# The bias of the output projection moved from a TensorE product with a row of ones to an add on GpSimd

## The chip, the cores and the metric

One Trainium2 chip, of which the kernel uses one core. The time is device microseconds of one execution. Engines are named as in the profile: PE is TensorE (PEld its weight loads), DVE is VectorE, ACT is ScalarE, POOL is GpSimd, SP is SyncE, which here only issues DMAs; PEq, SPq and so on are the engines' own queues.

## What is computed

A graph attention layer over 6250 nodes of 512 features and 100,000 edges (sorted by destination row), then a small feed-forward network, both with a residual. Cut to what matters here:

```python
edge_index = jnp.stack([src, dst])
x = x + _L0_gnn_ref(_layernorm(x), edge_index, edge_attr_8, Wq, bq, Wk, bk, Wv, bv, Wo, bo)
x = x + _L0_ffn_ref(_layernorm(x)[None], Wa, ba, Ws, bs)[0]

# in _L0_gnn_ref
q = (x @ Wq + bq).reshape(n, H, DK); k = (x @ Wk + bk)...; v = (x @ Wv + bv)...
logits = einsum('ehd,ehd->eh', q[rows] * scale, k[cols]) + att_bias
p = exp(logits - row_max[rows]);  att = p / denom[rows]
y = segment_sum(att[:, :, None] * v[cols], rows)
out = y.reshape(n, H * DK) @ Wo + bo
```

The feed-forward network reads a few thresholded features of each node (two rows of four numbers), sends them through two stacks of three layers of width 160, and adds rounded results into 33 of the 512 columns.

## The kernel before, in words

The nodes are cut into W = 49 windows of 128 rows (the last has 106). The work goes through stages in this order: the edges are read, turned into rows and counted per window (a histogram by products on PE), beside it q, k and v of the windows are computed and written to DRAM; the edges are sorted into tiles by scatter DMAs (POOL, L548); k rows are gathered for the logits (POOL, L561); v rows are gathered and summed per window (POOL, L571; PE L1661; DVE L1270); and last, per window, the result is normalized, projected, added to x, and sent through the feed-forward network. Each engine has its own instruction stream, written out by hand as nested functions in its block, and engines meet only through semaphores. The order on an engine is the order of the program text: there is no planner.

**The biases at the start.** SP loads bq, bk and bv as 32x16 pieces (L373) and bo (L374), then 38 small weights of the network (L382). DVE splits each bias into three bfloat16 terms whose sum is the float32 value (`split_bias`, L889 to L897), called at L916 and L917 for the two groups. SP copies the terms into rows on three partitions: nine DMAs for q, k, v (L403) and three for bo into `boS` (L407). The products of q, k and v on PE (L1530) each end with a product of a 3x128 tile of ones and those rows (L1533), which adds the bias in PSUM. Before the first of them PE waits for all twelve copies (L1532). Histogram products (L1541) and these units stand in one PE queue.

**The last stage.** SP loads Wo (L498) when the v stage is over, then x again for the first eight windows, into a ring of XR = 8 tiles `xr` (`f_load`, L503), and later stores pair g-1 and loads pair g+3 (`f_store`, L509). A load waits for the store that used its tile before. Windows are handled in pairs, g = 0 to 24. For each window:
- DVE `f_y` divides by the softmax sums (L1304 to L1311); PE `f_yT` transposes (L1683); ACT `f_yTe` copies (L752).
- PE `f_wo` makes four products of 128x512 with Wo (L1695) and ends with ones times `boS` (L1697), all into one PSUM bank.
- DVE `f_x1` adds the bank to x in place (L1318), after waiting for the product and for the load of x; `f_stats` takes mean and variance (L1325 to L1333), with a root on ACT (L783, `f_root`); `f_feats` writes the normalized row xn (L1356, L1363) and then some 14 small operations that end with the features as bfloat16 parts (L1368 to L1424).
- POOL `f_xs` adds xn to x in place (L577); this is all that POOL does in this stage.
- PE `f_fq` transposes the features (L1707), ACT copies them (L763); the layers are `f_h1` (L1715, ReLU on ACT L771), `f_h2` (L1725, ReLU L778) and `f_out` (L1739), which has four columns per product and runs 24 of them per pair.
- DVE `f_posts` (L1442 to L1475) rounds and adds into x, and SP stores.

The PE order of a pair stands at the end of the block. `f_wo` is called with a range of its five steps (0 to 3 the Wo products, 4 the bias), so that those steps of the pair after next stand between the layers of this pair: for the first window (0,1), (1,3), (3,5) behind the three parts of `f_h1`, for the second (0,2) behind `f_h2`, then `f_fq` of the next pair, and (2,3), (3,4), (4,5) behind the first three of four `f_out` parts. Every product in float32 runs as two instructions in the profile. On DVE the order in pair g is x1, statistics, posts of g-1, features of g+1, and `f_y` of g+4.

Of the kernel before, what the change touches and what calls it, by code (L numbers as in the profile page):

```python
# [17 lines left out]
def build(nc, x, src, dst, attr, wq, bq, wk, bk, wv, bv, wo, bo, waT, ba, wsT, bs, out):  # L18
# [4 lines left out]
    W = 49  # L23
# [18 lines left out]
    with ctx:  # L42
# [67 lines left out]
        Bt = [ar(3 * 48, bf16).rearrange("p (r n) -> p r n", r=3) for _ in range(2)]  # L110
        Bf = [ar(48) for _ in range(2)]
        Br = [ar(48) for _ in range(2)]
# [26 lines left out]
        boS = f_(512, bf16)  # L139
# [165 lines left out]
        w16 = e_(64).rearrange("p (a n) -> p a n", a=4)  # L305
        G = (W + 1) // 2
        s_ftz, s_wo = sem("s_ftz"), sem("s_wo")
        s_xt = sems("s_xt", XR // 2)
# [18 lines left out]
        def _(e):  # L327
# [44 lines left out]
            for i, b_ in enumerate((bq, bk, bv)):  # L372
                e.dma_start(Bf[0][0:32, 16 * i:16 * i + 16], b_.rearrange("(p n) -> p n", n=16)).then_inc(s_bl, 16)  # L373
            e.dma_start(Bf[1][0:32, 0:16], bo.rearrange("(p n) -> p n", n=16)).then_inc(s_bl, 16)  # L374
# [26 lines left out]
            for i in range(3):  # L401
                for j in range(3):
                    e.dma_start(Bs[i:i + 1, 512 * j:512 * j + 512].rearrange("a (p n) -> a p n", n=16),  # L403
                                Bt[0][0:32, i, 16 * j:16 * j + 16]).then_inc(s_brow, 16)
            q.wait_ge(s_bv, 8)
            for i in range(3):
                e.dma_start(boS[i:i + 1, 0:512].rearrange("a (p n) -> a p n", n=16), Bt[1][0:32, i, 0:16]).then_inc(s_brow, 16)  # L407
# [90 lines left out]
            e.dma_start(WoS, wo.rearrange("(c p) n -> p c n", p=128)).then_inc(s_wo, 16)  # L498

# [26 lines left out]
        def _(e):  # L526
# [52 lines left out]
            for w in range(W):  # L579
                f_xs(w)  # L580
# [232 lines left out]
        def _(e):  # L813
# [75 lines left out]
            def split_bias(k, n, bf, br, bt):  # L889

                e.tensor_copy(bt[0:32, 0, 0:n], bf[0:32, 0:n]).then_inc(s_bv, 1)
                q.wait_ge(s_bv, 4 * k + 1)
                e.tensor_tensor(br[0:32, 0:n], bf[0:32, 0:n], bt[0:32, 0, 0:n], ALU.subtract).then_inc(s_bv, 1)
                q.wait_ge(s_bv, 4 * k + 2)
                e.tensor_copy(bt[0:32, 1, 0:n], br[0:32, 0:n]).then_inc(s_bv, 1)
                q.wait_ge(s_bv, 4 * k + 3)
                e.tensor_tensor(bt[0:32, 2, 0:n], br[0:32, 0:n], bt[0:32, 1, 0:n], ALU.subtract).then_inc(s_bv, 1)  # L897
# [11 lines left out]
            for c in range(NCH + AHEAD):  # L909
                if c == 12:  # L910
                    e.memset(stV[:, :, 64:65], 1.0).then_inc(s_cv, 1)
                if c == 32:
                    ln_stats(0)
                    ln_out(0)
                    q.wait_ge(s_bl, 64)
                    split_bias(0, 48, Bf[0], Br[0], Bt[0])  # L916
                    split_bias(1, 16, Bf[1], Br[1], Bt[1])  # L917
# [396 lines left out]
            def f_x1(w):  # L1314
                n, k, xx = rows_of[w], w % 2, xr[w % XR]
                q.wait_ge(s_fo, w + 1)
                q.wait_ge(s_xt[w // 2 % 4], 32 * (w // XR) + 16 * len(pair(w // 2)))
# [183 lines left out]
        def _(e):  # L1501
# [9 lines left out]
            def unit(u):  # L1511
# [20 lines left out]
                q.wait_ge(s_brow, 12 * 16)  # L1532
# [154 lines left out]
            def f_wo(w, c0=0, c1=5):  # L1687
# [3 lines left out]
                q.wait_ge(s_brow, 12 * 16)  # L1691
                q.wait_ge(s_x1, w - 1)
                for c in range(c0, c1):
                    if c < 4:
                        e.matmul(BK[1 + k][0:n, :], yT[w % 4][:, c, 0:n], WoS[:, c, :], start=(c == 0), stop=False)  # L1695
                    else:
                        e.matmul(BK[1 + k][0:n, :], ones[0:3, 0:n], boS[0:3, :], start=False, stop=True).then_inc(s_fo, 1)  # L1697
# [59 lines left out]
            for g in range(G):  # L1757
# [5 lines left out]
                if n2:  # L1763
                    f_wo(n2[0], 1, 3)
                f_h1(g, 2)
                if n2:
                    f_wo(n2[0], 3, 5)
# [7 lines left out]
                if len(n2) > 1:  # L1775
                    f_wo(n2[1], 0, 2)
# [3 lines left out]
                if len(n2) > 1:  # L1780
                    f_wo(n2[1], 2, 3)
                f_out(g, (1,))
                if len(n2) > 1:
                    f_wo(n2[1], 3, 4)
                f_out(g, (2,))
                if len(n2) > 1:
                    f_wo(n2[1], 4, 5)
# [28 lines left out]
```

## Time and profile before

| what | value |
|---|---|
| median of 3 runs | 3968.57 us (3964.55 to 3970.23) |
| profiled execution | 3972.73 us, span 3970.9 us |
| granted clock of PE, mean over the span | 0.929 |
| busy: PE, DVE, POOL, ACT | 82%, 77%, 64%, 40% |
| the last stage | 3392 to 3971 us |
| L1697, product with ones, in the last stage | 49, one of 128x512 drawn with 385 ns |
| L577, add on POOL | 49, mean 1382 ns |

Times are microseconds from the start of the span. A row of a timeline has the start, the length, the engine, the line of the kernel, the operation, the tiles (R, fw, small are large tiles of SBUF, banks is PSUM) and the count of instructions put together; in brackets stands how long the engine had been idle before it and who released it. PE's products overlap and their ends are modelled, so the step from one start to the next says what a product costs. The granted clock is a fraction of full speed: 1.00 is 2.4 GHz, 0.50 is 1.2 GHz. "issue" is a wait for nothing that the profile shows.

### The profile page before, as it was taken

Reading aid. Unit: us, or ns where it says so; the run is one execution under the profiler, and the core shown is the slowest. Engines: PE = TensorE matmul, PEld = TensorE weight load, DVE = VectorE, ACT = ScalarE, POOL = GpSimd, SP = SyncE. Lnnn points to the kernel's source line nnn. Section 1 sums busy time; section 2 is a strip of 40 time slices with the busy share of each in tenths; the row PEclk is TensorE's granted clock in tenths of the full one; section 3 lists DMA queues with packets and bytes.
Section 4 is the critical chain, followed back from the end, with each engine's and each line's share of the span. In section 5 each row is a group of like instructions: output and inputs, shape, how many; then the busy total and the mean of one; then the engine's idle time right before and its main releaser. Section 6 shows DMA issues by size and latency. Waiting matters only on the chain. (4 is left out here: it accounts for less than half of the span.)

```text
span 3970.9 us, 46880 instructions
## 1 busy us (share of the span) xinstructions
PE 3251.2 (82%) x12499; PEld 1740.2 (44%) x12499; DVE 3046.2 (77%) x7930; ACT 1569.7 (40%) x3864; POOL 2531.8 (64%) x2586
## 2 busy tenths in 40 slices
PE   5799898888824777777777688888888888899998
PEld 3455454444411222222222266665566655344443
DVE  7676666666625999999999888888888888565654
ACT  4443333333302222222222267777677776222222
POOL 4377777777775777777777777777777777011110
PEclk8899898888957999999999989999999999899998
DMA  5243343333337777777777868888888788211111
GB/s 146 80 128 113 97 112 104 100 105 101 102 117 240 233 241 235 235 237 237 238 237 238 211 200 229 238 235 235 229 231 234 234 235 204 68 48 43 53 43 37
DMA packets 280166, 663.66 MB, mean 167 GB/s; under 512 B 85022, under 2 KB 88934, under 8 KB 279652
## 3 DMA queue, kind: packets, MB, share of 16 engines
q0 software_dynamic: 158144, 443.78, 39.4%
q1 hardware_dynamic: 115416, 204.10, 16.3%
q10 hardware_dynamic: 6348, 12.80, 0.9%
q8 instruction: 106, 1.74, 0.2%
q14 instruction: 152, 1.25, 0.1%
HBM read 599.96 MB, written 60.50 MB: 166 GB/s over the span
## 5 line engine op out<-in xcount | busy, mean ns | idle before, releaser
L1661 PE MATMUL banks<-R,small 128*128 128x260 f32 x3328 | 894.4, 408 | 156.3 <-DVE R L1257 138.0
L571 POOL DMA_INDIRECT R<-v_scratch,dstS x832 | 829.2, 997 | 262.0 <-issue 159.7
L561 POOL DMA_INDIRECT R<-k_scratch,dstS x832 | 791.9, 952 | 291.1 <-issue 261.3
L548 POOL DMA_INDIRECT rec_scratch<-R,small x782 | 770.5, 985 | 282.9 <-issue 237.4
L1603 PE MATMUL banks<-R,small 128*128 x1664 | 799.5, 614 | 184.9 <-DVE R L1114 149.2
L1661 PEld LDWEIGHTS banks<-R,small 128*128 128x128 f32 x3328 | 593.4, 195 | 404.3 <-DVE R L1257 313.4
L731 ACT ACTIVATE R<-R 128x65 f32<-128x65 f32 x2496 | 663.1, 339 | 268.3 <-DMA R<-v_scratch,dstS 263.7
L1530 PE MATMUL banks<-R 128*128 128x512 f32 (+1 forms) x1176 | 610.9, 668 | 62.0 <-ACT R L597 61.8
L1270 DVE TENSOR_TENSOR R<-R,banks 128x520 f32 x832 | 571.2, 686 | 24.2 <-PE banks L1661 18.3
L1603 PEld LDWEIGHTS banks<-R,small 128*128 128x128 f32 x1664 | 292.2, 191 | 653.1 <-issue 653.1
L1114 DVE TENSOR_TENSOR R<-banks,R 128x1024 f32<-128x1024 f32 x416 | 503.8, 1211 | 79.8 <-DMA R<-k_scratch,dstS 43.1
L1121 DVE TENSOR_REDUCE R<-R 128x16 f32<-128x1024 f32 x416 | 502.1, 1207 | 0.0
L1257 DVE TENSOR_TENSOR R<-R 128x325 f32<-128x325 f32 x832 | 407.0, 489 | 108.2 <-DMA R<-v_scratch,dstS 106.2
L686 ACT ACTIVATE small<-rowR,npidx 128x1024 f32<-128x1024 bf16 x104 | 119.5, 1149 | 804.1 <-PE banks L1603 776.6
L1530 PEld LDWEIGHTS banks<-R 128*128 128x128 f32 (+1 forms) x1176 | 239.4, 214 | 321.5 <-issue 254.8
L577 POOL TENSOR_TENSOR R<-R 128x512 f32<-128x512 f32 (+1 forms) x49 | 66.8, 1380 | 491.4 <-DVE R L1363 491.4
L608 ACT ACTIVATE R<-banks 128x512 f32<-128x512 f32 (+1 forms) x147 | 87.9, 598 | 554.3 <-PE banks L1533 554.3
L1003 DVE SCALAR_TENSOR_TENSOR R<-R 128x128 f32<-128x128 uint16 x782 | 268.1, 344 | 7.8 <-DMA R<-src_rows 7.8
L1565 PE MATMUL banks<-R 128*128 128x49 f32 x1564 | 208.4, 302 | 68.2 <-issue 38.3
L1043 DVE SCALAR_TENSOR_TENSOR small<-R 128x8 int32<-128x8 f32 x98 | 16.3, 167 | 309.4 <-DMA rec_scratch<-R,small 309.4
L1695 PE MATMUL banks<-R 128*128 128x512 f32 (+1 forms) x392 | 232.6, 704 | 3.0 <-DMA R<-in_L_gnn_Wo_dram 1.6
L1565 PEld LDWEIGHTS banks<-R 128*128 128x128 f32 x1564 | 195.1, 203 | 88.5 <-issue 56.5
(226 smaller groups left out, 3228.1 us busy)
## 6 DMA issues: line engine op xcount, KB each, us to landing
rowR<-lo_sorted SPq DMA_DIRECT2D x104, 512.0 KB, 5.8
rowR<-lo_rows SPq DMA_DIRECT2D x97, 256.0 KB, 3.9
R<-src_rows SPq DMA_DIRECT2D x97, 256.0 KB
R<-in_x_dram SPq DMA_DIRECT2D x96, 256.0 KB, 2.9
R<-k_scratch,dstS POOLq DMA_INDIRECT x832, 3.9
R<-v_scratch,dstS POOLq DMA_INDIRECT x832, 3.9
rec_scratch<-R,small POOLq DMA_INDIRECT x782
v_scratch<-R SPq DMA_DIRECT2D x48, 260.0 KB
```

The costliest lines, as they stand in the source:

```text
L548: e.indirect_dma_start(recd, bass.IndirectOffsetOnAxis(ap=ridx[:, c % 4, j:j + 1], axis=0), rec[:, 8 * c + j, :], None).then_inc(s_sc[c % ...
L561: e.indirect_dma_start(Kr[t // 2 % (KR // 2)][:, 512 * (t % 2):512 * (t % 2) + 512], None, Kd, bass.IndirectOffsetOnAxis(ap=dstS[:, t:t + ...
L571: e.indirect_dma_start(Vr[t % VR], None, Vd, bass.IndirectOffsetOnAxis(ap=dstS[:, t:t + 1], axis=0)).then_inc(s_v2[t % VR], 16)
L731: ins = e.activation(heads(Vr[t % VR], h, h + 1), heads(Vr[t % VR], h, h + 1), ACT.Copy, scale=ph[:, h:h + 1])
L1114: e.tensor_tensor(Kr[i % (KR // 2)], QB[i % 3], Kr[i % (KR // 2)], ALU.mult).then_inc(s_pr, 1)
L1121: e.tensor_reduce(flat(Lr[k][:, 2 * (i % 8):2 * (i % 8) + 2, :]), Kr[i % (KR // 2)].rearrange("p (h d) -> p h d", d=64), AX.X, ALU.add).th ...
L1257: e.tensor_tensor(heads(Vr[t % VR], 0, HA2), heads(Vr[t % VR], 0, HA2), ph[:, 0:HA2].rearrange("p (h a) -> p h a", a=1).broadcast_to([128, ...
L1270: e.tensor_tensor(yw, yw, YB[t % 3].rearrange("p (q n) -> p q n", q=2)[:, :, 0:260], ALU.add).then_inc(s_ya, 1)
L1530: e.matmul(bank[0:n, :], xT[w % 2][:, c, 0:n], W3[m][:, c, :], start=(c == 0), stop=False)
L1565: ins = e.matmul(BK[GK[c % 3]][:, j * W:(j + 1) * W], AT[c % 3][:, j, :], Cs[c % 3][:, :, j], start=True, stop=True)
L1603: e.matmul(QB[t // 2 % 3][:, 512 * (t % 2):512 * (t % 2) + 512], ohT[(t // 8) % 2][:, t % 8, :], Qall[:, bass.ds(e.snap(win[t % 16], min_v ...
L1661: ins = e.matmul(YB[t % 3][:, 512 * i:512 * i + 260], o, Vr[t % VR][:, 260 * i:260 * i + 260], start=True, stop=True)
```

## The change

The product of ones and `boS` goes from `f_wo`, and with it the load, the split and the three copies of bo. The bias is loaded once in the last stage, spread over 128 partitions, into `boB`, a part of the tile `small` that is free by then; SP issues this DMA between Wo and the loads of x. POOL adds `boB` to each x tile (`f_xb`) as soon as the load has landed, two pairs ahead in its own order: the adds of pair 0, then for each g those of pair g+1 followed by `f_xs` of pair g. `f_x1` on DVE waits for that add instead of the load. `f_wo` has four steps, and its calls in the loop are cut anew. PE's wait before the first product of q, k, v is for nine copies. The tiles `Bt`, `Bf`, `Br` are one each, so that what is carved behind them in R2 lies 168 words lower.

```diff
-        Bt = [ar(3 * 48, bf16).rearrange("p (r n) -> p r n", r=3) for _ in range(2)]
-        Bf = [ar(48) for _ in range(2)]
-        Br = [ar(48) for _ in range(2)]
+        Bt = ar(3 * 48, bf16).rearrange("p (r n) -> p r n", r=3)
+        Bf = ar(48)
+        Br = ar(48)
...
-        boS = f_(512, bf16)
...
+        boB = small[:, 512:1024]
+        s_bo, s_xb = s_bl, s_bv
...
-            e.dma_start(Bf[1][0:32, 0:16], bo.rearrange("(p n) -> p n", n=16)).then_inc(s_bl, 16)
...
-            q.wait_ge(s_bv, 8)
-            for i in range(3):
-                e.dma_start(boS[i:i + 1, 0:512].rearrange("a (p n) -> a p n", n=16), Bt[1][0:32, i, 0:16]).then_inc(s_brow, 16)
...
             e.dma_start(WoS, wo.rearrange("(c p) n -> p c n", p=128)).then_inc(s_wo, 16)
+            e.dma_start(boB, bo.rearrange("(a n) -> a n", a=1).broadcast_to([128, 512])).then_inc(s_bo, 16)
...
-            for w in range(W):
-                f_xs(w)
+            def f_xb(w):
+
+                n = rows_of[w]
+                q.wait_ge(s_bo, 48 + 16)
+                q.wait_ge(s_xt[w // 2 % 4], 32 * (w // XR) + 16 * len(pair(w // 2)))
+                e.tensor_tensor(xr[w % XR][0:n, :], xr[w % XR][0:n, :], boB[0:n, :], ALU.add).then_inc(s_xb, 1)
+
+            for w in pair(0):
+                f_xb(w)
+            for g in range(G):
+                for w in pair(g + 1):
+                    f_xb(w)
+                for w in pair(g):
+                    f_xs(w)
...
-                    split_bias(0, 48, Bf[0], Br[0], Bt[0])
-                    split_bias(1, 16, Bf[1], Br[1], Bt[1])
+                    q.wait_ge(s_bl, 48)
+                    split_bias()
...
-                q.wait_ge(s_xt[w // 2 % 4], 32 * (w // XR) + 16 * len(pair(w // 2)))
+                q.wait_ge(s_xb, 4 + w + 1)
                 e.tensor_tensor(xx[0:n, :], xx[0:n, :], BK[1 + k][0:n, :], ALU.add).then_inc(s_x1, 1)
...
-                q.wait_ge(s_brow, 12 * 16)
+                q.wait_ge(s_brow, 9 * 16)
...
-            def f_wo(w, c0=0, c1=5):
+            def f_wo(w, c0=0, c1=4):
...
-                q.wait_ge(s_brow, 12 * 16)
                 q.wait_ge(s_x1, w - 1)
                 for c in range(c0, c1):
-                    if c < 4:
-                        e.matmul(BK[1 + k][0:n, :], yT[w % 4][:, c, 0:n], WoS[:, c, :], start=(c == 0), stop=False)
-                    else:
-                        e.matmul(BK[1 + k][0:n, :], ones[0:3, 0:n], boS[0:3, :], start=False, stop=True).then_inc(s_fo, 1)
+                    ins = e.matmul(BK[1 + k][0:n, :], yT[w % 4][:, c, 0:n], WoS[:, c, :], start=(c == 0), stop=(c == 3))
+                if c1 == 4:
+                    ins.then_inc(s_fo, 1)
...
                 if n2:
-                    f_wo(n2[0], 1, 3)
+                    f_wo(n2[0], 1, 2)
                 f_h1(g, 2)
                 if n2:
-                    f_wo(n2[0], 3, 5)
+                    f_wo(n2[0], 2, 4)
...
                 if len(n2) > 1:
-                    f_wo(n2[1], 0, 2)
+                    f_wo(n2[1], 0, 1)
                 if n1:
                     f_fq(g + 1)
                 f_out(g, (0,))
                 if len(n2) > 1:
-                    f_wo(n2[1], 2, 3)
+                    f_wo(n2[1], 1, 2)
                 f_out(g, (1,))
                 if len(n2) > 1:
-                    f_wo(n2[1], 3, 4)
+                    f_wo(n2[1], 2, 3)
                 f_out(g, (2,))
                 if len(n2) > 1:
-                    f_wo(n2[1], 4, 5)
+                    f_wo(n2[1], 3, 4)
                 f_out(g, (3,))
```

## Rows read from the trace of the kernel before

**Rows 1.** Busy time of TensorE over the span, from the page.
```profile
PE 3251.2 (82%) x12499; PEld 1740.2 (44%) x12499; DVE 3046.2 (77%) x7930; ACT 1569.7 (40%) x3864; POOL 2531.8 (64%) x2586
```

**Rows 2.** Window of 20 pairs: length, PE, PEld, DVE, ACT, POOL, clock, DMA.
```profile
3439.40:3886.20 446.80, 446.80 (x1422) 192.33 (x1422) 266.67 (x1317) 120.08 (x240) 54.62 (x40) 0.94 0.14 48
```

**Rows 3.** Waits, 3400 to 3900 us: us in total, times, longest.
```profile
DVE R L1318 <- PE banks L1697: 140.5, 21, 7.7
...
PE banks L1683 <- ACT R L752: 1.5, 2, 0.8
```

**Rows 4.** Timeline of PE, one pair at full clock: start, length, what.
```profile
3663.64 0.40 PE L1707 MATMUL banks<-small,R 128*36 128x128 bf16 x4
...
3668.24 0.38 PE L1697 MATMUL banks<-fw,ones 3*128 3x512 bf16 x1
3668.56 0.92 PE L1739 MATMUL banks<-fw,R 128*128 128x4 f32 x6
...
3684.60 0.40 PE L1707 MATMUL banks<-small,R 128*36 128x128 bf16 x4
```

**Rows 5.** Timeline of PE: where a pair begins, five of 25 times.
```profile
3439.44 0.40 PE L1707 MATMUL banks<-small,R 128*36 128x128 bf16 x4
...
3462.06 0.40 PE L1707 MATMUL banks<-small,R 128*36 128x128 bf16 x4
...
3486.21 0.40 PE L1707 MATMUL banks<-small,R 128*36 128x128 bf16 x4
...
3507.17 0.40 PE L1707 MATMUL banks<-small,R 128*36 128x128 bf16 x4
...
3886.18 0.40 PE L1707 MATMUL banks<-small,R 128*36 128x128 bf16 x4
```

**Rows 6.** Two windows of that stage (columns as in Rows 2).
```profile
3639.40:3645.00 5.60, 5.60 (x33) 4.14 (x32) 0.53 (x1) 0.63 (x2) 0.00 (x0) 1.00 0.00 0
3645.00:3651.80 6.80, 6.80 (x10) 2.18 (x10) 4.18 (x25) 1.38 (x2) 0.00 (x0) 0.50 0.21 80
```

**Rows 7.** Timeline of DVE in the pair of Rows 4, and at the end.
```profile
3674.18 0.26 DVE L1356 RECIPROCAL small<-small 128x1 f32<-128x1 f32 x2 [0.80 <-ACT small L783]
...
3675.30 2.51 DVE L1368 SCALAR_TENSOR_TENSOR R<-R 128x64 f32<-128x64 f32 x2
...
3680.02 0.28 DVE L1424 TENSOR_TENSOR R<-R 128x24 bf16<-128x24 f32 x2
...
3932.39 0.23 DVE L1368 SCALAR_TENSOR_TENSOR R<-R 106x64 f32<-106x64 f32 x1
3932.53 1.23 DVE L1372 TENSOR_SCALAR R<-R 106x3 f32<-106x3 f32 x1
```

**Rows 8.** Timeline of POOL, SP's queue and ACT in that pair.
```profile
3675.01 2.72 POOL L577 TENSOR_TENSOR R<-R 128x512 f32<-128x512 f32 x2 [18.21 <-DVE R L1363]
...
3673.28 0.82 SPq L509 DMA_DIRECT2D out_dram<-R  x2
3675.99 0.81 SPq L503 DMA_DIRECT2D R<-in_x_dram  x2
...
3682.80 0.68 ACT L778 ACTIVATE R<-banks,fw 64x512 f32<-64x512 f32 x1 [2.27 <-PE banks L1725]
```

**Rows 9.** Start of the stage: DVE's last features, PE's first transposes.
```profile
3419.53 0.28 DVE L1424 TENSOR_TENSOR R<-R 128x24 bf16<-128x24 f32 x2
...
3421.29 0.40 PE L1707 MATMUL banks<-small,R 128*36 128x128 bf16 x4
```

**Rows 10.** Start of the kernel: SP's queue, PE's first row-of-ones product.
```profile
32.46 0.42 SPq L374 DMA_DIRECT2D R<-in_L_gnn_bo_dram  x1
...
59.62 5.70 SPq L403 DMA_DIRECT2D R<-R  x9
65.36 1.85 SPq L407 DMA_DIRECT2D fw<-R  x3
...
68.47 0.58 PE L1533 MATMUL banks<-R,ones 3*128 3x512 bf16 x1 [9.10 <-DMA fw<-R]
```

More of the change, by code:

```diff
@@ L372, in _ @@
             for i, b_ in enumerate((bq, bk, bv)):
-                e.dma_start(Bf[0][0:32, 16 * i:16 * i + 16], b_.rearrange("(p n) -> p n", n=16)).then_inc(s_bl, 16)
-            e.dma_start(Bf[1][0:32, 0:16], bo.rearrange("(p n) -> p n", n=16)).then_inc(s_bl, 16)
+                e.dma_start(Bf[0:32, 16 * i:16 * i + 16], b_.rearrange("(p n) -> p n", n=16)).then_inc(s_bl, 16)
             q.wait_ge(s_iota, 5)
@@ L403, in _ @@
                     e.dma_start(Bs[i:i + 1, 512 * j:512 * j + 512].rearrange("a (p n) -> a p n", n=16),
-                                Bt[0][0:32, i, 16 * j:16 * j + 16]).then_inc(s_brow, 16)
-            q.wait_ge(s_bv, 8)
-            for i in range(3):
-                e.dma_start(boS[i:i + 1, 0:512].rearrange("a (p n) -> a p n", n=16), Bt[1][0:32, i, 0:16]).then_inc(s_brow, 16)
+                                Bt[0:32, i, 16 * j:16 * j + 16]).then_inc(s_brow, 16)
             for k_ in range(NCH):
@@ L887, in unit, with split_bias @@
                     ln_out(w + 1)
[L889 to L897, printed above, removed]
+            def split_bias():
+                e.tensor_copy(Bt[0:32, 0, :], Bf[0:32, :]).then_inc(s_bv, 1)
+                q.wait_ge(s_bv, 1)
+                e.tensor_tensor(Br[0:32, :], Bf[0:32, :], Bt[0:32, 0, :], ALU.subtract).then_inc(s_bv, 1)
+                q.wait_ge(s_bv, 2)
+                e.tensor_copy(Bt[0:32, 1, :], Br[0:32, :]).then_inc(s_bv, 1)
+                q.wait_ge(s_bv, 3)
+                e.tensor_tensor(Bt[0:32, 2, :], Br[0:32, :], Bt[0:32, 1, :], ALU.subtract).then_inc(s_bv, 1)
             def build_A(c, sm_):
@@ L914, in _ @@
                     ln_out(0)
-                    q.wait_ge(s_bl, 64)
-                    split_bias(0, 48, Bf[0], Br[0], Bt[0])
-                    split_bias(1, 16, Bf[1], Br[1], Bt[1])
+                    q.wait_ge(s_bl, 48)
+                    split_bias()
                 if c < NCH:
```

## Prediction, made before the changed kernel ran

> **What bounds the kernel now.** I began with the page: TensorE is the busiest engine at 82% [rows 1], but that is an average over stages with different limits, so the stages that the change touches have to be read one by one. They are two: the last stage, from about 3392 us, where the output projection is computed, and the first 70 us, where the bias is split and copied. Between them the gathers run, which the change leaves alone.
>
> In the last stage the windows view shows PE busy for all of 446.80 us while it goes through 20 pairs of windows; DVE is busy for 60% of that, POOL for 12% [rows 2]. The list of waits agrees: DVE waits 140.5 us for PE's row-of-ones product, and the longest sum that PE itself waits for anybody is 1.5 us [rows 3]. So the stage costs what PE's queue costs.
>
> The PE timeline gives the price of one pair. From one L1707 to the next, at full clock, it is 20.96 us (3663.64 to 3684.60); the product with the row of ones starts at 3668.24 and the next instruction at 3668.56, so it takes 0.32 us of the queue, and not the 0.38 that it is drawn with [rows 4]. The starts of L1707 also show that pairs are not all alike: 22.62, then 24.15, then 20.96 [rows 5]. Of the 20, nine are of 20.96, five of about 22.6, six of about 24.2, together 446.74. The windows view says why. Between 3639.4 and 3645.0 PE runs the transposes of features and 24 four-column products, with two Wo products and one bias product between them, all at clock 1.00; behind it, from 3645.0 to 3651.8, the granted clock is 0.50, the lower of its two levels, 1.2 GHz instead of 2.4, on products of full width [rows 6]. It then returns to 1.00. Over the 20 pairs these falls cost 446.7 - 20 x 20.96 = 27.5 us. Each of the falls follows such a run of small products.
>
> **The change part by part.**
>
> *The product goes.* 49 row-of-ones products by 0.32 us [rows 4] are 15.7 us, all on the queue that bounds the stage. A little is unsafe: a run of Wo products at the place of the bias also saves the change of shape, so up to 0.4 us each, 19.6; the low end is nothing for those in the first pairs. I take 15.7. What could come late in its place are the ACT copies that PE needs; each has at least as many PE instructions in front of it as before except the last ReLU of the second layer, which is left with one Wo product and the four transposes of L1707, more than 1 us together, over an ACT operation of 0.68 us [rows 8]. That covers it.
>
> [...]
>
> *The Wo products are spread anew.* The second window of a pair now has one product ahead of L1707 instead of two, and three between the four groups of small products instead of two and the bias. At full clock that is neutral. But it puts a full-width product where the clock falls from: 24 small products now have three wide ones among them, and nothing thin. In the run of rows 6 PE then has half as much wide work again. The price at one end is nothing, if the clock falls as before; at the other all of the 27.5 us [rows 5, 6], with every pair at 20.96 - 0.64 = 20.3 us. There is no row of a pair with three. I take the far end, because already with two products nine of the 20 pairs stay at full clock, and half as much wide work again is a large step.
>
> *POOL's new adds.* 49 adds of 128x512 at half of 2.72 us each [rows 8] are 67 us on an engine that is busy for 12% of the stage. Its own time is hidden. What isn't, is what it does to DVE: L1368 takes 2.51 us for two while POOL adds, 0.23 for one when POOL has not begun, and then it is the next one, L1372 with three columns, that takes 1.23 [rows 7]. So a POOL add holds a DVE operation until the add is over. Two more adds per pair can hold DVE 2.7 us more. Where they fall: the queue puts them behind the adds of xn of the pair two before, and they wait for x, whose load is issued at 3675.99, behind the stores [rows 8], so they start near 3679, when DVE is at the end of the features. These end at 3680.0 + 0.3, and PE wants them at 3684.60 [rows 4, 7]: 4.3 us of slack. At 20.3 us a pair, and with the bias gone, about 3.9 remain, over 2.7. DVE as a whole has 40% idle. I cost it at nothing in the 20 pairs; if that cover were gone, each 0.1 us is 2 us.
>
> In front of them it isn't covered. For the first pairs x is loaded early, so four adds run in a row while DVE makes the first features; these end at 3419.8 and PE takes them at 3421.29 [rows 9]. PE would be there 1.3 us sooner without four bias products, and DVE 2.6 us later less 0.6 that it too gains. PE waits, and the next Wo product, which waits for DVE's x1, is late as well: a loss of 3.3 us against the sum above (bounds 0 and 5).
>
> *Waits and queues.* x1 on DVE now waits for POOL instead of for the load; the add was done a pair earlier. Behind a waiting add stands the add of xn of the next pair, which has some 15 us left. On SP one DMA of 256 KB stands between Wo and the x loads, whose first use is 15 us on; it delays them by one issue, 0.4 us. Nothing.
>
> *The start.* SP issues one load of bo (0.46 us with its step to the next), nine copies of the split biases, and three copies for the output bias in 1.85 us; PE's first row-of-ones product waits 9.10 us for the last of those three, and with it everything stands [rows 10]. Without them the wait ends 2.3 us earlier. PE is then busy without a gap, so most is passed on: 2.3, bounds 0 and 3.
>
> *Sum:* 15.7 + 27.5 - 3.3 + 2.3 = 42.2 us, against the profiled execution's 3972.73 (span 3970.9, 1.8 outside it): 3930.5. That execution lies 4.2 us above the median of the three runs, 3968.57, so in terms of the median 3926.4.
>
> **The rivals.**
>
> *The clock falls as often as before* (that the change does only what its words say, remove a product). The four-column products all stay, and the falls may hang on them rather than on the wide products between them. Then 42.2 - 27.5 = 14.7 us: 3954. If half of the falls stay, 3940.
>
> *POOL holds DVE until PE waits (slower).* Place: L1707 waiting for the features. For: L1368 above, already held for 2.2 of its 2.5 us. It decides from 3.9 us more per pair. If the two adds and what they hold stretch each other to twice the length, 5.5 us, PE waits 1.6 in each of 22 pairs, 35 us; and an idle PE ahead of the small products brings the clock's falls back, 27.5. Then -42.2 + 62.7 = 20 us slower: 3989. Against it: the adds start late in the features, and the present ones keep to 1.36 us beside DVE.
>
> The rule behind this is in the Trainium skill, "GPSIMD Engine Reference", section "Specifications": the SBUF interfaces are shared with VectorE, with contention for DVE operations that have two SBUF inputs or a two-port mode. By that rule L1368 is held, and the trace agrees at 1.26 us each.
>
> *The falls go but DVE's hold costs some:* 0.5 us a pair, 11 us: 3938.
>
> **How the numbers follow.** The forecast, all falls gone or nearly, 0.68; half of them or DVE's hold of some tenths, 0.13; all falls stay, 0.12; PE waits for features and the clock falls, slower, 0.05; the rest, nearly no change, 0.02. The forecast's own range is 3918 to 3936 from the bounds above and a spread of the runs of 3 us each way; the second group takes it to 3945, and 0.19 is left out. A measurement of this kernel can tell about 0.2%, 8 us; all cases but the last two are beyond it.
>
> **What would show it.** Right: from L1707 to L1707 20.3 us for nearly all of the 20 pairs, the clock at 1.00 in them, no L1697, PE busy throughout, DVE ahead of PE at L1707, and PE's first L1533 at about 66.2. Wrong: pairs of 23 us, so the clock; an idle time of PE in front of L1707 with DVE as its releaser; POOL adds longer than 1.4 us.

## The result, and the profile after

The changed kernel takes **3918.82 us** (four runs, 3914.05 to 3921.2); the kernel before, beside it, 3966.56 us (3959.53 to 3970.23). The ratio is 0.9879, with an interval of 0.9867 to 0.9891: 47.7 us less, 4.8 us more or less. That is the direction that was forecast and in the range, near its lower end and 7.6 us below the 3926.4 us of the sum. The profiled execution took 3920.09 us, against 3972.73 us before.

The later experiments ran in three groups and one single run, each with the kernel before beside it. In the last two groups and the single run, on other chips, the stages of gathers and scatters were slower, so that the kernel before took 4564, 4589 and 4630 us there; why is not known. Their whole times are compared only within a group, and their last stage, which isn't slower there (536.1 and 536.4 us for the changed kernel on two chips), by its trace. A ratio is worked out within a group from its runs and is not the quotient of the two medians beside it; its interval (95%) is what to go by.

The page, as in [rows 1]:

```profile
PE 3206.7 (82%) x12450; PEld 1734.8 (44%) x12450; DVE 3079.0 (79%) x7926; ACT 1567.4 (40%) x3864; POOL 2594.0 (66%) x2635
```

PE is busy for 44.5 us less, POOL for 62 us more. Three stretches of the last stage in the windows view (length, PE, PEld, DVE, ACT, POOL with their counts, clock, DMA share, GB/s): from the load of Wo to the second pair, the 20 pairs, the rest.

```profile
3381.70:3429.90 48.20, 37.57 (x95) 15.16 (x95) 32.23 (x118) 11.13 (x21) 15.27 (x12) 0.86 0.20 71
3429.90:3833.40 403.50, 403.50 (x1382) 183.00 (x1382) 299.05 (x1318) 120.01 (x240) 111.80 (x80) 1.00 0.15 53
3833.40:3918.20 84.80, 72.61 (x225) 34.50 (x224) 34.14 (x185) 17.70 (x37) 8.01 (x6) 0.76 0.08 30
```

The middle line answers to [rows 2]: the 20 pairs take 403.5 us instead of 446.8, PE is still busy in all of it, and the granted clock is 1.00 instead of 0.94. No pair shows 0.50 any more. POOL is busy for 112 us instead of 55, in 80 adds instead of 40, and DVE for 299 instead of 267, though its work is the same: the 32 us more are operations held while POOL adds.

The timeline of PE at three places: the first product with ones, the start of the last stage, and one pair, to be held against [rows 4, 9, 10]:

```profile
65.41 0.58 PE L1542 MATMUL banks<-R,ones 3*128 3x512 bf16 x1 [6.25 <-DMA R<-R]
...
3410.51 0.40 PE L1714 MATMUL banks<-small,R 128*36 128x128 bf16 x4 [1.31 <-DVE R L1433]
...
3413.30 2.07 PE L1702 MATMUL banks<-R 128*128 128x512 f32 x2 [1.27 <-DVE R L1327]
...
3571.13 0.40 PE L1714 MATMUL banks<-small,R 128*36 128x128 bf16 x4
...
3572.31 1.13 PE L1702 MATMUL banks<-R 128*128 128x512 f32 x2
...
3574.02 1.13 PE L1702 MATMUL banks<-R 128*128 128x512 f32 x2
...
3575.73 1.13 PE L1702 MATMUL banks<-R 128*128 128x512 f32 x2
...
3591.30 0.40 PE L1714 MATMUL banks<-small,R 128*36 128x128 bf16 x4
```

The pair takes 20.17 us (3571.13 to 3591.30), against 20.96. All 20 pairs do. Three Wo products stand between the four-column ones, each two instructions. The two rows at 3410 and 3413 us have what [rows 9] did not: PE waits 1.31 us for DVE's features and 1.27 us for x1. The product with ones at the start begins at 65.41 us instead of 68.47.

The list of waits over the 20 pairs (us in total, times, longest):

```profile
DVE R L1327 <- PE banks L1702: 99.7, 20, 6.0
...
POOL R L583 <- DMA R<-in_x_dram: 54.5, 20, 3.6
```

The same 20 pairs of the kernel before have

```profile
DVE R L1318 <- PE banks L1697: 132.8, 20, 6.6
```

(the 140.5 us of [rows 3] are of a longer window). So DVE's wait for the projection fell from 132.8 to 99.7 us, and it is still the largest of DVE: DVE has room. POOL waits for the load of x in each pair, so its adds of the bias begin when x has landed and no sooner. Where that falls shows in the timelines of DVE and then of POOL, in the pair of the rows above:

```profile
3576.89 0.69 DVE L1327 TENSOR_TENSOR R<-R,banks 128x512 f32<-128x512 f32 x1 [4.92 <-PE banks L1702]
...
3587.34 0.28 DVE L1433 TENSOR_TENSOR R<-R 128x24 bf16<-128x24 f32 x2
...
3587.97 0.69 DVE L1320 TENSOR_TENSOR R<-R 128x512 f32<-128x512 f32 x1
3588.58 1.23 DVE L1313 TENSOR_SCALAR R<-R 128x8 f32<-128x8 f32 x1
3589.85 0.20 DVE L1316 RECIPROCAL R<-R 128x8 f32<-128x8 f32 x1
3590.09 1.47 DVE L1320 TENSOR_TENSOR R<-R 128x512 f32<-128x512 f32 x1
```

```profile
3582.33 2.72 POOL L576 TENSOR_TENSOR R<-R 128x512 f32<-128x512 f32 x2 [11.96 <-DVE R L1372]
3588.10 2.91 POOL L583 TENSOR_TENSOR R<-R,small 128x512 f32<-128x512 f32 x2 [3.05 <-DMA R<-in_x_dram]
```

The features end at 3587.34 + 0.28 and PE wants them at 3591.30: 3.7 us of slack. The bias adds start at 3588.10, half a us behind the features. That is a thin margin: in 19 of the 20 pairs they start between 0.1 us before the end of the features and 1.0 us behind it, and in one they start inside the last feature operation:

```profile
3647.86 1.39 DVE L1433 TENSOR_TENSOR R<-R 128x24 bf16<-128x24 f32 x2
...
3647.94 2.52 POOL L583 TENSOR_TENSOR R<-R,small 128x512 f32<-128x512 f32 x2 [2.37 <-DMA R<-in_x_dram]
```

There the features end 1.1 us late, at 3649.25, and PE, which wants them at 3651.83, still does not wait. So it is the slack that covers the adds, and not only their place. What they hold in the pair above is the `f_y` of a later pair: a TENSOR_SCALAR of 8 columns takes 1.23 us instead of 0.17, a TENSOR_TENSOR 1.47 instead of 0.69. The RECIPROCAL between them takes its usual 0.20.

Where the time went, from the trace of each, in us (the last stage counts from the issue of the Wo load to the end):

| | before | after | difference |
|---|---|---|---|
| Wo load to the first of the 20 pairs | 47.22 | 48.15 | +0.9 |
| the 20 pairs | 446.74 | 403.47 | -43.3 |
| behind them | 84.72 | 84.81 | +0.1 |
| the last stage | 578.64 | 536.43 | -42.2 |
| Wo load issued at | 3392.2 | 3381.8 | -10.4 |

The last line can't be read as an effect of the change; the first experiment shows what it is worth.

### The profile page after: what moved, and what is told of

Its sections match the earlier page's. It is cut to its first block and busy times, and to the rows that moved or that the text cites. A ratio compares the mean times of both kernels' runs of the same rounds, so it can differ in the third digit from the quotient of the medians.

```text
span 3918.2 us, 46849 instructions
## 1 busy us (share of the span) xinstructions
PE 3206.7 (82%) x12450; PEld 1734.8 (44%) x12450; DVE 3079.0 (79%) x7926; ACT 1567.4 (40%) x3864; POOL 2594.0 (66%) x2635
## 5 line engine op out<-in xcount | busy, mean ns | idle before, releaser
L1539 PE MATMUL banks<-R 128*128 128x512 f32 (+1 forms) x1176 | 604.8, 663 | 59.8 <-ACT R L608 59.7
L1123 DVE TENSOR_TENSOR R<-banks,R 128x1024 f32<-128x1024 f32 x416 | 503.7, 1211 | 77.9 <-DMA R<-k_scratch,dstS 42.2
L1702 PE MATMUL banks<-R 128*128 128x512 f32 (+1 forms) x392 | 215.8, 649 | 4.6 <-DVE R L1327 2.7
```

Of the source, the lines that this page charges most:

```text
L1123: e.tensor_tensor(Kr[i % (KR // 2)], QB[i % 3], Kr[i % (KR // 2)], ALU.mult).then_inc(s_pr, 1)
L1539: e.matmul(bank[0:n, :], xT[w % 2][:, c, 0:n], W3[m][:, c, :], start=(c == 0), stop=False)
L1702: ins = e.matmul(BK[1 + k][0:n, :], yT[w % 4][:, c, 0:n], WoS[:, c, :], start=(c == 0), stop=(c == 3))
```

## The experiments

**The kernel before, once more** (no edit).

> The kernel before once more, unchanged, to see how far its stages differ between two traces. Theory: the last stage repeats within 1 us (578.6), the start within 0.3 us, and the gather stages of k and v (1079.5 us from the last scatter to the first gather of v, less the rest, and 1105.1 from there to Wo) differ by several us, so that the 8 us by which the changed kernel was shorter in them are no effect of the change. Rival: they repeat within 1 us, and the 8 us need a cause.

Measured: 3970.48 us, median of 10, against 3968.35 of 21; ratio 1.0001 (0.9991 to 1.0011). SP's queue in its trace:

```profile
3380.51 0.39 SPq L498 DMA_DIRECT2D R<-in_L_gnn_Wo_dram  x1
```

So two traces of one kernel differ by 11.7 us before the last stage begins (3392.2 and 3380.5), more than the 10.4 us of the table, which are therefore no evidence. The last stage is steadier: 579.77 us. Its 20 pairs sum to 441.97: again 20.96 where undisturbed, but ten pairs with a fall of the clock, for 22.8 us, where the first trace had eleven, for 27.5. A third trace with this order of products in the last stage, that of the start alone below, has eleven again, for 29.1 us, and a last stage of 581.8 us. So what the falls cost varies from trace to trace, between 22.8 and 29.1 us here.

**The Wo products spread as in the change, the bias product kept.**

```diff
-                    f_wo(n2[0], 1, 3)
+                    f_wo(n2[0], 1, 2)
...
-                    f_wo(n2[0], 3, 5)
+                    f_wo(n2[0], 2, 5)
...
-                    f_wo(n2[1], 0, 2)
+                    f_wo(n2[1], 0, 1)
...
-                    f_wo(n2[1], 2, 3)
+                    f_wo(n2[1], 1, 2)
...
-                    f_wo(n2[1], 3, 4)
+                    f_wo(n2[1], 2, 3)
...
-                    f_wo(n2[1], 4, 5)
+                    f_wo(n2[1], 3, 5)
```

> The kernel before, with the product of ones kept, but the Wo products of a pair spread as in the changed kernel: one ahead of the feature transposes, three between the groups of four-column products. Theory A (the clock falls because the run of small products has too little wide work in it): most falls go though nothing is taken from PE; pairs of about 21.1 us (20.96 and 0.1 to 0.2 for one more change of shape), 20 pairs in 422 to 434 us instead of 446.7, so 3942 to 3955 us against 3966. Rival B (the falls went because the bias product went, or because POOL now delays something): pairs as before or worse, 20 pairs in 446 us or more, time within 5 us of the kernel before or slower.

Measured: 3958.29 us, ratio 0.9966 (0.9954 to 0.9979). PE's timeline, three starts of a pair:

```profile
3434.65 0.40 PE L1707 MATMUL banks<-small,R 128*36 128x128 bf16 x4
...
3457.41 0.40 PE L1707 MATMUL banks<-small,R 128*36 128x128 bf16 x4
...
3478.57 0.40 PE L1707 MATMUL banks<-small,R 128*36 128x128 bf16 x4
```

One pair with a fall, 22.76 us, and one without, 21.16. Six of 20 are of the first kind (three of 22.76, three of 24.35), and the sum is 437.5: 14.3 us of falls are left, where the three traces of the old order have 22.8 to 29.1: about half. Spreading alone works, but not fully: the sum is above the 422 to 434 us that were expected, and the time above the 3942 to 3955 us, though its interval (3950 to 3960) reaches into them. The undisturbed pair is 0.2 us longer than before, as expected.

**The product gone, the Wo products placed as before**, and nothing where the bias stood.

```diff
-                    f_wo(n2[0], 1, 2)
+                    f_wo(n2[0], 1, 3)
...
-                    f_wo(n2[0], 2, 4)
+                    f_wo(n2[0], 3, 4)
...
-                    f_wo(n2[1], 0, 1)
+                    f_wo(n2[1], 0, 2)
...
-                    f_wo(n2[1], 1, 2)
+                    f_wo(n2[1], 2, 3)
...
-                    f_wo(n2[1], 2, 3)
+                    f_wo(n2[1], 3, 4)
                 f_out(g, (2,))
-                if len(n2) > 1:
-                    f_wo(n2[1], 3, 4)
                 f_out(g, (3,))
```

(the lines are against the changed kernel)

> The changed kernel (no product of ones, bias added by POOL), but the Wo products placed as before: two ahead of the feature transposes, two between the groups of four-column products, nothing in the place of the bias. Theory A: the falls of the clock come back in about half of the pairs, undisturbed pairs of 20.1 us, 20 pairs in 415 to 425 us, so 12 to 22 us slower than the changed kernel (3931 to 3941). Rival B: no falls, 20 pairs in 403 us, the time of the changed kernel.

Measured: 3945.5 us, ratio 0.9935 (0.9918 to 0.9952). PE's timeline, one pair with a fall and one without:

```profile
3444.18 0.40 PE L1714 MATMUL banks<-small,R 128*36 128x128 bf16 x4
...
3467.55 0.40 PE L1714 MATMUL banks<-small,R 128*36 128x128 bf16 x4
...
3476.85 1.12 PE L1702 MATMUL banks<-R 128*128 128x512 f32 x2
3477.81 0.60 PE L1692 MATMUL banks<-ident,R 128*128 128x128 f32 x4
3478.25 4.18 PE L1732 MATMUL banks<-R,fw 128*128 128x512 f32 x8
...
3487.72 0.40 PE L1714 MATMUL banks<-small,R 128*36 128x128 bf16 x4
```

and the place in front of the transposes in the kernel before, in the pair of [rows 4]:

```profile
3673.26 1.13 PE L1695 MATMUL banks<-R 128*128 128x512 f32 x2
3674.32 0.39 PE L1697 MATMUL banks<-fw,ones 3*128 3x512 bf16 x1
3674.64 0.65 PE L1683 MATMUL banks<-ident,R 128*128 128x128 f32 x4
3675.13 1.02 PE L1725 MATMUL banks<-R,fw 128*128 128x512 f32 x2
```

The undisturbed pair is 20.17 us, exactly that of the changed kernel, but the one before it takes 23.37. Nine of 20 have a fall, for 22.7 us, at the low end of what the old order shows (22.8 to 29.1). The 20 pairs take 426.1 us, just above the expected 415 to 425. So the removal alone leaves the falls about where they were, and the two edits aren't additive. Apart from the falls the removal alone brings 15.8 us in the pairs. With the falls, and against the three traces of the old order (442.0 to 448.3 us), the removal alone brings 16 to 22 us, the spread alone 4 to 11, both together 38 to 45. The whole times agree: the spread alone is 10 us below the kernel before, the removal alone 23, both together 48, more than the sum of the two.

These rows also tell why a product is worth more than 0.32. At the place in front of the transposes, two Wo instructions, the bias and the first transposes take 3675.13 - 3673.26 = 1.87 us; without the bias 3478.25 - 3476.85 = 1.40: 0.47 saved, because the Wo product before it and the transposes behind it each take less when nothing thin stands between them. At the other place, among four-column products, the remaining 0.32 is saved, as [rows 4] had it. The sum is the 0.79 us by which a pair is shorter.

**The start alone**: in the kernel before, the first product with ones waits for the nine copies, and the three of the output bias are waited for in the last stage.

```diff
-                ... .then_inc(s_brow, 16)
+                ... .then_inc(s_bro, 16)
...
-                q.wait_ge(s_brow, 12 * 16)
+                q.wait_ge(s_brow, 9 * 16)
...
-                q.wait_ge(s_brow, 12 * 16)
+                q.wait_ge(s_bro, 3 * 16)
```

> The kernel before, with one edit: PE's first product of ones waits for the nine copies of the q, k, v biases alone, and the three copies of the output bias, issued as before, are waited for in the last stage. Theory: this product starts 1.9 us earlier, at about 66.6 instead of 68.5, and the scatters start about 1.5 to 2 us earlier than 171.3; the last stage takes 578 to 579 us as before. The time changes by 1 to 3 us, less than the runs differ. Rival: the histogram stage takes the time back elsewhere and the scatters start at 171 as before.

Measured: 3968.7 us, ratio 1.0 (0.999 to 1.001). PE's first product with ones:

```profile
66.17 0.58 PE L1534 MATMUL banks<-R,ones 3*128 3x512 bf16 x1 [6.32 <-DMA R<-R]
```

It comes 2.3 us sooner (1.9 were expected), and the whole time shows nothing of it. The scatters start at 169.8 us, as expected, but in the traces of the unchanged kernel they start at 171.3 and 168.6, so that is no evidence either. The traces say why the gain can't be read: from this product to the last histogram product PE takes 71.1 to 71.5 us in the traces where the clock is 0.50 for about 16 us of it (before, this one, after), and 67.5 us where it is 0.50 for about 8 us (the copy of before and the spread alone). That difference in the clock comes with 4 us here, more than the gain. The last stage took 581.8 us, not the expected 578 to 579, with 29.1 us of falls.

**Each bias add computed twice**, the additional one into scratch; **and four times.**

```diff
+                for i in range(1 * w, 1 * w + 1):
+                    q.wait_ge(s_z2, i - 2)
+                    e.tensor_tensor(Z2[i % 3][0:n, :], xr[w % XR][0:n, :], boB[0:n, :], ALU.add).then_inc(s_z2, 1)
```

(three in place of each 1 for four times)

> The changed kernel, and POOL computes each bias add twice, once more into a scratch tile, so that it may hold DVE 2.9 us longer in a pair. In the changed kernel the adds start when the features are already done, hold DVE's division of a later pair instead, and DVE still idles 4.9 us in a pair of 20.17. Theory: PE stays busy throughout, 20 pairs in 403 to 405 us, DVE's idle time before x1 falls from 4.9 to about 2; in front of the first pairs, where four adds stood in a row, 2 to 5 us more, so 3921 to 3926. Rival (POOL's adds already bear on the time): 20 pairs longer by 10 us or more.

> The changed kernel with each bias add computed four times, three of them into scratch tiles: some 8.7 us more per pair in which POOL may hold DVE, against 4.9 us of idle DVE and 3.7 us between the last feature and PE's use of it. Theory: DVE becomes the bound, pairs of about 23 to 25 us, PE idle ahead of the feature transposes, clock falls back as well, so 60 to 110 us slower than the changed kernel. Rival: DVE isn't held for all of POOL's time, and the pairs stay under 21 us.

Measured, twice: 4510.99 against 4564.32 us, ratio 0.9958 (0.9901 to 1.0014), which tells nothing from the kernel before; last stage 539.2 us, the pairs 403.5 as in the changed kernel and the 2.8 us more in front of them and within the 2 to 5 expected. POOL's timeline:

```profile
4201.04 1.27 POOL L587 TENSOR_TENSOR small<-R,small 128x512 f32<-128x512 f32 x1 [2.91 <-DMA R<-in_x_dram]
4202.26 1.71 POOL L588 TENSOR_TENSOR R<-R,small 128x512 f32<-128x512 f32 x1
4203.94 1.26 POOL L587 TENSOR_TENSOR small<-R,small 128x512 f32<-128x512 f32 x1
4205.17 1.72 POOL L588 TENSOR_TENSOR R<-R,small 128x512 f32<-128x512 f32 x1
```

Four adds now, from 4201.04 to 4206.9, and DVE's features of that pair had ended at 4200.7: here the adds still come behind them. In the 20 pairs they start between 0.1 us before the end of the features and 2.0 us behind it. 55 us more of POOL in 20 pairs cost none there.

Measured, four times: 4771.68 us, ratio 1.0493 (1.0191 to 1.0794). The last stage takes 795.3 us, 259 more than in the changed kernel where 60 to 110 were expected, and a pair 30 to 32. DVE's, POOL's and PE's timelines in one pair, then the window behind PE's wait:

```profile
4305.03 1.31 DVE L1386 TENSOR_SCALAR R<-R 128x3 f32<-128x3 f32 x2
4306.26 0.33 DVE L1390 TENSOR_REDUCE R<-R 128x4 f32<-128x64 f32 x2
...
4307.49 1.31 DVE L1397 TENSOR_SCALAR R<-R 128x4 f32<-128x4 f32 x2
4308.72 1.30 DVE L1401 TENSOR_TENSOR R<-R 128x1 f32<-128x1 f32 x2
...
4315.62 0.28 DVE L1438 TENSOR_TENSOR R<-R 128x24 bf16<-128x24 f32 x2
```

```profile
4302.31 2.72 POOL L578 TENSOR_TENSOR R<-R 128x512 f32<-128x512 f32 x2 [19.52 <-DVE R L1377]
4304.99 3.72 POOL L587 TENSOR_TENSOR small<-R,small 128x512 f32<-128x512 f32 x3
...
4313.55 1.26 POOL L588 TENSOR_TENSOR R<-R,small 128x512 f32<-128x512 f32 x1
```

```profile
4315.86 0.61 PE L1719 MATMUL banks<-small,R 128*36 128x128 bf16 x4 [3.68 <-DVE R L1438]
```

```profile
4315.80:4332.90 17.10, 17.04 (x41) 9.32 (x41) 7.36 (x34) 2.01 (x4) 0.00 (x0) 0.50 0.07 26
```

This is the slower rival in full. POOL doesn't wait for x between its adds any more: the longer pair has given the load time to land, so the adds stand right behind `f_xs`, inside the features. Operations of one to four columns take 1.3 us for two, where they take 0.23 undisturbed: the first of each is held until a POOL add is over. The features are late, PE waits 3.68 us, and the products behind this wait run at clock 0.50 for all of the 17.1 us. The expected size, 23 to 25 us a pair, was too small by 5 to 9: the features are held for some 8 us, PE's wait and the clock lengthen the pair further, and a longer pair leaves the loads time to land, so that the adds stay in the worse place. Which of these came first was not tested.

**No bias add at all.** The output bias is left out of the result; POOL adds nothing for it, and x1 waits for the load.

```diff
-            for w in pair(0):
-                f_xb(w)
...
-                for w in pair(g + 1):
-                    f_xb(w)
...
-                q.wait_ge(s_xb, 4 + w + 1)
+                q.wait_ge(s_xt[w // 2 % 4], 32 * (w // XR) + 16 * len(pair(w // 2)))
```

> The changed kernel without POOL's bias adds: the output bias is left out of the computation, and x1 waits for the load of x again. Theory: the falls of the clock depend on PE's order alone and the adds cost nothing behind the first pairs, so 20 pairs in 403.5 us at clock 1.00 as with the adds; in front of them the waits of PE go, and the last stage takes 533 to 534 us, as with the adds up front. Rival (POOL's adds have a part in the clock or in the pairs): 20 pairs differ by 2 us or more from 403.5, or the stage takes under 531.

One run: 4550.86 us, beside 4629.66 of the kernel before. Its 20 pairs in the windows view (columns as above):

```profile
4060.70:4464.10 403.40, 403.40 (x1381) 182.71 (x1380) 264.95 (x1317) 120.13 (x240) 55.00 (x40) 1.00 0.15 53
```

DVE is busy for 265 us instead of 299, and the pairs take 403.4 us all the same. So the adds cost nothing in the pairs, and the falls did not go because of what POOL does: as long as PE does not wait, its own order decides. (Where PE does wait, as with four adds, the clock falls too.) In front of the pairs 45.1 us stand against 48.15: the adds cost 3 us there. The last stage is 533.3 us, in the 533 to 534 expected. One whole time beside one tells nothing more.

**The bias adds of the first three pairs ahead of everything** on POOL, run twice.

```diff
-            for w in pair(0):
+            for w in pair(0) + pair(1) + pair(2):
...
-                for w in pair(g + 1):
-                    f_xb(w)
+                if g >= 2:
+                    for w in pair(g + 1):
+                        f_xb(w)
```

> The changed kernel, with POOL's bias adds of the first three pairs done up front, while POOL has nothing else to do, instead of the third pair's behind the first two adds of xn. Theory: DVE isn't held while it makes the first features, PE's waits of 1.3 us each at the first feature transposes and at the next Wo product go, and the last stage takes 533 to 535 us instead of 536.4, in the 20 pairs nothing changes. The time changes by 1 to 3 us. Rival: other waits of the first pairs stand right behind those and the stage takes 536.

Measured: 4530.6 against 4564.32 us, ratio 0.9936 (0.9883 to 0.999); last stage 533.22 us. PE's timeline at the start of the stage, with the line numbers one up:

```profile
4027.38 0.40 PE L1715 MATMUL banks<-small,R 128*36 128x128 bf16 x4
...
4029.62 1.13 PE L1703 MATMUL banks<-R 128*128 128x512 f32 x2 [0.58 <-DVE R L1328]
```

No wait at the transposes, 0.58 us at the next Wo product instead of 1.27, and 45.08 us to the first of the 20 pairs: the same 3 us, won back.

**The same, and the small products grouped more tightly**: the three parts of `f_h1` behind one another, two Wo products before them and two behind; and between the four-column products one Wo product, then two, with the last two parts of `f_out` in one.

```diff
-                f_h1(g, 0)
                 if n2:
-                    f_wo(n2[0], 0, 1)
-                f_h1(g, 1)
-                if n2:
-                    f_wo(n2[0], 1, 2)
-                f_h1(g, 2)
+                    f_wo(n2[0], 0, 2)
+                for k_ in range(3):
+                    f_h1(g, k_)
                 if n2:
                     f_wo(n2[0], 2, 4)
...
-                    f_wo(n2[1], 2, 3)
-                f_out(g, (2,))
-                if len(n2) > 1:
-                    f_wo(n2[1], 3, 4)
-                f_out(g, (3,))
+                    f_wo(n2[1], 2, 4)
+                f_out(g, (2, 3))
```

> The kernel before it (bias adds of the first pairs up front) with fewer changes of shape in PE's order of a pair: the three products of the first layer stand together between two and two Wo products, and between the four-column groups stand one and two Wo products, the last two groups together. The Wo products still stand on both sides of the small products. Theory: 19.7 us a pair instead of 20.17 at full clock, 20 pairs in 393 to 396 us if the clock doesn't fall; about 10 us faster than the changed kernel, 3905 to 3912. Rival: the small products are less well mixed with wide ones and the clock falls in some pairs, 20 pairs in 400 to 415.

Measured: 4519.53 us, ratio 0.9915 (0.9859 to 0.9971); last stage 527.43 us. Its 20 pairs:

```profile
4044.00:4443.00 399.00, 399.00 (x1381) 184.48 (x1380) 307.05 (x1317) 115.46 (x240) 105.31 (x80) 1.00 0.16 53
```

19.96 us a pair, at clock 1.00, where 19.7 were expected: 0.21 saved for five changes of shape. By PE's timeline all of it comes from the first layer, where three changes fewer save 0.28 us (4.88 to 4.60 us from its start to the transposes), while the four-column part with two changes fewer takes 0.07 more (5.91 to 5.98). Three wide products placed as one and two keep the clock up as three single ones did.

**The three versions side by side**, in one group.

> The changed kernel once more, unchanged, beside the next two. Theory: the last stage takes 536 to 539 us, its 20 pairs 403.5 us with the clock at 1.00; what the whole kernel gains over the one before in the same company is 1.0 to 1.3%. Rival (the gain seen first was partly chance): under 0.8%.

> The bias adds of the first three pairs up front, in the same company as the unchanged one. Theory: the last stage takes 533 us, 3 us less than the changed kernel's; in the whole time that is 0.08%, which these rounds can't tell from no change. Rival: the stage takes 536 us or more here.

> The early adds and the fewer changes of shape, in the same company. Theory: 20 pairs in 399.2 us with the clock at 1.00, the last stage in 526 to 529 us, 8 to 10 us faster than the changed kernel and 1.3 to 1.6% faster than the kernel before. Rival: the clock falls in some pairs at another phase, 20 pairs in 402 us or more.

| | median, us | ratio to before (4589.09) | last stage, us |
|---|---|---|---|
| the changed kernel | 4552.04 | 0.9945 (0.9908 to 0.9982) | 536.12 |
| adds early | 4540.62 | 0.9914 (0.9879 to 0.9948) | 533.39 |
| early and grouped | 4557.74 | 0.9946 (0.9912 to 0.9979) | 527.20 |

All three are faster than before; among them the whole times can't tell, as single runs of one kernel lie 80 to 140 us apart here. The gains of the whole kernel missed what was expected: the changed kernel is 0.2 to 0.9% faster here, not 1.0 to 1.3%, which is the side of the rival (under 0.8%), and even the upper end, 42 us, is below the 47.7 of the first result; the grouped one is 0.2 to 0.9% faster, not 1.3 to 1.6%. The last stage of the changed kernel is as short as before in its trace, so the difference would lie in the stages in front or in how far single runs scatter; no trace of the kernel before was kept on this chip, and it stays open. The last stage repeats to 0.3 us (536.43 and 536.12, 533.22 and 533.39, 527.43 and 527.20). There the grouped version is 9 us shorter than the changed kernel; that the whole kernel is faster by so much wasn't shown.

## Why the prediction was right, and where it was off

- **The product's price** was the term mis-sized. Forecast: 49 by 0.32 = 15.7 us. In the 20 pairs alone 40 of them brought 0.79 a pair, 15.8 us, or 0.395 each, where 40 by 0.32 are 12.8; the saved change of shape that the prediction named for its upper bound of 0.4 is what it did not take. That all 49 are "on the queue that bounds the stage" did not hold: behind the pairs, where four of them stood, nothing is gained (84.72 to 84.82), as PE is busy for only 72.61 of the 84.80 us there. What the five in front of the pairs brought isn't separated from the clock. The Trainium skill ("TensorE: Matmul & The Clock Gate", "Back-to-back issue gap") gives N/2.4 + 2.5 ns for an isolated product, 216 ns at 512 columns, and about 131 ns for one in a stream. By its larger figure 49 products would be an estimate of 10.6 us. This trace disagrees with both: the product stands between other shapes and costs 0.32 us in one place and 0.47 in the other.
- **The clock's falls**: forecast 27.5 us, all gone. 446.74 - 403.47 - 15.8 = 27.5. The reason given, more wide work among the small products and nothing thin, is borne out in part. The rival that the falls hang on the small products alone is out: these are all still there. (The "24 four-column products" of a pair are 12 products, of two instructions each; the Wo products among them were counted as products, so it is 12 beside two or three.) But the spread alone left half of the falls and the removal alone nearly all of them; the prediction had no row that showed the two together would end them, so that none is left was in part luck. So is the size: the 27.5 come from one trace, and the other two of the same order have 22.8 and 29.1. Whether the thin product matters as such, or by the time that it adds to the small ones, wasn't separated.
- **POOL beside DVE**: forecast nothing in the pairs; measured nothing, since without any add the pairs take 403.4 us as well. The slack was put at 3.9 us and is 3.7. The adds were placed a little over 1 us before the end of the features, with what they hold to be paid out of that slack; they start at about the end and mostly hold `f_y`, which nobody waits for. Only in one pair did they use the slack, 1.1 us of it. The adds take 1.42 us on average in place of the 1.36 assumed. "POOL adds longer than 1.4 us" was named as a sign of being wrong: it came, by a little, and meant nothing for the time.
- **In front of the pairs**: forecast a loss of 3.3 us; 3.07 by the run with early adds (48.15 - 45.08), and 3.00 by the second pair of traces (48.98 - 45.98). The places were right too: 1.31 us at the first transposes and 1.27 at the next Wo product.
- **The start**: forecast 2.3 us; the product came 2.3 us sooner with the wait alone, 3.06 in the changed kernel, which also lacks the load and the split of bo. The last histogram product, from 139.9 to 136.6 us in two traces with equally long stretches at clock 0.50, agrees with its being passed on; the whole time is too coarse to show it.
- **The sum**: for the last stage 15.7 + 27.5 - 3.3 = 39.9 us forecast, 42.2 measured. Against the other two traces of the old order it would be 43 to 45. Of the 47.7 us of the medians, 42.2 are this stage and about 3 the start. The remaining 2.5 are inside the interval of 4.8 and stay unexplained.
- **The range**: by the bounds named, its lower end is 3968.57 - 19.6 - 27.5 - 3.0 = 3918.5, without the 3 us for the spread of the runs that the upper end has; with them it would be 3915. The measured 3918.82 lies just inside even so. And the slower case, at 3989, would also have been told from no change by 8 us; only the last case would not.
- **The slower rival**, POOL holding DVE until PE waits, exists, but not here: POOL has four operations in a pair in the changed kernel, the doubled add makes them six and costs PE nothing, the fourfold one makes them ten and costs 10 to 12 us a pair. Its price had been worked out without the feedback.

## What to carry to other kernels

On a PE-bound stage count what a thin product costs in its queue with its neighbours, from two traces or from the steps around it, and then look at the granted clock: here the falls of the clock that went with both edits together were worth more than the product removed. Work given to an idle engine is free only for as long as it falls behind the operations that the bounding engine waits for; find what times it (here the landing of x) and how far that can move.

## What the runs showed of the hardware

- PE's clock falls to 0.50 while PE is never idle. Before the change this came behind a run of small products (transposes of features and 12 four-column products, 24 instructions) and cost 22.8 to 29.1 us of 20 pairs in three traces; with three Wo products among them and no thin one it did not happen in any of 20 pairs, in six traces of this order and two of the grouped one.
- DVE operations of a few columns are held for about 1.2 us while POOL adds 128x512 elements: TENSOR_SCALAR, COPY, TENSOR_TENSOR and SCALAR_TENSOR_TENSOR are, RECIPROCAL (0.20 us) and TENSOR_REDUCE (0.33 us for two, at 4306.26 above) are not. The Trainium skill, "GPSIMD Engine Reference", "Specifications", names operations with two SBUF inputs or in a two-port mode; the held TENSOR_TENSOR and SCALAR_TENSOR_TENSOR have both inputs in SBUF and agree with the first, and no run here shows the mode of the others. A TENSOR_TENSOR with one input in PSUM is not held (0.67 us at 4205.68, beside an add, with two adds computed). POOL's adds lengthen as well: 1.26 us, but 1.71 where a DVE operation of 128x512 that the add before had held is still running (4202.26, with two adds computed; that DVE operation runs from 4201.06 to 4202.85).
- Two traces of one kernel lie 11.7 us apart ahead of the last stage. That stage lay between 578.6 and 581.8 us in three traces of the old order, with its falls of the clock, and repeats to 0.3 us in the new one, without them.
